# The output gate's state half, formed once and added by VectorE in each batch

## The reference

```
xn = layernorm(x)
x + attention(xn) + cell(xn)

# attention: qkv = xn @ W_qkv + b_qkv, 16 heads of 64, softmax(q k / 8) v, then @ W_out + b_out
# cell: the 8 batches are its time steps, the 512 rows its batch
def step(c, xt):
    ft = sigmoid(xt @ wf.T + c @ uf.T + bf)
    it = sigmoid(xt @ wi.T + c @ ui.T + bi)
    gt = tanh(xt @ wc.T + c @ uc.T + bc)
    return ft * c + it * gt
c_final = scan(step, in_c, xn)
h = tanh(xn @ wo.T + c_final @ uo.T + bo)      # for every time step, with the last state
```

## Time and profile before

| | us |
|---|---|
| median of 3 runs | 822.47 |
| lowest to highest | 821.98 to 822.47 |
| the profiled execution | 821.97 |
| its span in the profile | 820.2 |
| PE busy in it | 811.3 |
| POOL busy | 651.7 |
| DVE busy | 554.4 |
| ACT busy | 481.0 |

### The profile page before, as it was taken

One profiled execution on the slowest core, in us unless ns is written; L12 is line 12 of the kernel. 1 busy time (PEld: TensorE's weight loads), 2 busy tenths in 40 slices (PEclk: granted clock), 3 DMA queues, 4 the chain that ended last, 5 costly groups with the idle time before them and its releaser, 6 DMA issues.

```text
span 820.2 us, 15666 instructions
## 1 busy us (share of the span) xinstructions
PE 811.3 (99%) x5443; PEld 482.3 (59%) x5443; DVE 554.4 (68%) x733; ACT 481.0 (59%) x642; POOL 651.7 (79%) x361
## 2 busy tenths in 40 slices
PE   8899999999999999999999999999999999999998
PEld 5556655575555655556555555557555555666554
DVE  6779768775877647665676657676576757676545
ACT  5646866565556646664666636665566636666352
POOL 4938898895687859887798859988598869988595
PEclk9999999999999999999999999999999999999999
DMA  8102121221101101100001000010001000030010
GB/s 257 53 28 79 28 79 40 53 79 27 41 2 41 28 2 16 35 7 26 1 14 40 1 27 14 1 39 27 1 14 40 1 26 1 14 79 15 2 17 24
DMA packets 81430, 27.00 MB, mean 33 GB/s; under 512 B 63314, under 2 KB 75120, under 8 KB 81392
## 3 DMA queue, kind: packets, MB, share of 16 engines
q1 hardware_dynamic: 81062, 26.35, 13.2%
q10 hardware_dynamic: 330, 0.15, 0.1%
HBM read 16.79 MB, written 8.39 MB: 31 GB/s over the span
## 4 chain that ended last, share of the span: by engine, by line
PE 96%; POOL 1%; ACT 1%; DMA 1%; DVE 0%; ACTq 0%; issue 0%; POOLq 0%
PE st L1048 21%; PE misc L1062 14%; PE pv L1062 14%; PE st L986 10%; PE mx L1034 8%; PE st L1054 7%; PE mx L1100 5%; PE st L1091 4%; PE misc L969 3%; PE mx L969 3%; PE misc L986 3%; PE pv L986 3%; POOL PSUMK L421 1%; POOL PSUMK L428 1%; DMA probs<-in_L_ffn_in_c_dram 1%; PE st L1122 0%
## 5 line engine op out<-in xcount | busy, mean ns | idle before, releaser
L732 DVE TENSOR_REDUCE NM<-mx 128x2 f32<-128x1024 f32 x256 | 313.9, 1226 | 165.0 <-PE mx L1034 165.0
L540 ACT ACTIVATE probs<-st 128x1024 f32<-128x1024 f32 x256 | 256.5, 1026 | 53.6 <-PE st L1054 47.2
L415 POOL TENSOR_TENSOR PSUMK<-probs 128x1024 f32<-128x1024 f32 x64 | 154.1, 2408 | 31.7 <-ACT probs L540 31.7
L421 POOL TENSOR_TENSOR PSUMK<-PSUMK,probs 128x1024 f32<-128x1024 f32 x64 | 153.1, 2392 | 6.6
L428 POOL TENSOR_TENSOR PSUMK<-PSUMK,probs 128x1024 f32<-128x1024 f32 x63 | 151.0, 2396 | 6.4
L407 POOL TENSOR_TENSOR AL<-U,AH 128x512 fp32r<-128x512 f32 x60 | 77.2, 1287 | 81.0 <-ACT AH L532 81.0
L1062 PE MATMUL misc<-probs,VALL 128*64 128x512 f32 x512 | 122.4, 599 | 0.0
L1062 PE MATMUL pv<-probs,VALL 128*64 128x512 f32 x512 | 117.1, 599 | 0.0
L1034 PE MATMUL mx<-KH,QH 64*128 64x512 f32 x512 | 107.5, 413 | 2.0 <-DVE NM L732 1.7
L1048 PE MATMUL st<-QH,KH 64*128 64x512 f32 x512 | 104.0, 399 | 0.3 <-ACT probs L540 0.3
L1048 PE MATMUL st<-QH,KL 64*128 64x512 f32 x512 | 101.8, 390 | 0.0
(11 more groups left out here) (218 smaller groups left out, 1326.1 us busy)
## 6 DMA issues: line engine op xcount, KB each, us to landing
MROW<-TT SPq DMA_DIRECT2D x255, 1.0 KB
x_store<-XH SPq DMA_DIRECT2D x8, 256.0 KB, 2.1
x_store<-XL SPq DMA_DIRECT2D x8, 256.0 KB, 2.4
RX<-R SPq DMA_DIRECT2D x124, 2.0 KB, 1.7
xn_store<-XN SPq DMA_DIRECT2D x7, 256.0 KB, 2.5
XN<-xn_store SPq DMA_DIRECT2D x28, 64.0 KB, 2.3
XSH<-x_store SPq DMA_DIRECT2D x7, 256.0 KB, 2.8
XSL<-x_store SPq DMA_DIRECT2D x7, 256.0 KB, 2.9
```

Of the source, the lines that this page charges most:

```text
L415: nc.gpsimd.tensor_tensor(PSUMK[:, s % 2, :, :], e[:, :, 0, :], e[:, :, 1, :], ALU.add).then_inc(sum_part, 1)
L421: nc.gpsimd.tensor_tensor(PSUMK[:, s % 2, :, :], PSUMK[:, s % 2, :, :], probs[:, s % 2, :, 2, :], ALU.add).then_inc(sum_part, 1)
L540: nc.scalar.activation(probs[:, s % 2, :, u, :], st[:, u % 2, :, :], ACT.Exp, scale=SCALE).then_inc(exp_done, 1)
L732: nc.vector.tensor_reduce(NM[:, s % 2, 0:2 * TB].rearrange("p (h b) -> p h b", h=2)[:, :, b], mx[:, :, :], AX.X, ALU.max, negate=True).the ...
```

## The change

The three products of the output gate with the state are formed once, at the end of batch 1, behind that stretch's sums (`make_state_part`, into mx bank 1). ACT evacuates them with the gate's bias added into tile 0 of XN (`keep_state_part`, in ACT's program behind the last high part of that stretch), and PE waits for this (`part_kept`) before it goes on to the loop and writes mx again. A gate of h is now three matmuls with x alone (`output_gate`). DVE adds the kept array to misc in place (`add_state_part`), and the tanh waits for this addition (`h_added`) instead of the gate and has no bias of its own.

```diff
+        state_part = XN[:, 0, :, :].rearrange("p b d -> p (b d)")
...
             def tanh_h(count, out=OT):
-                act.wait_ge(h_done, count)
-                nc.scalar.activation(out[:, :], misc[:, :], ACT.Tanh, bias=bcol[:, B_O:B_O + 1]).then_inc(ht_done, 1)
+                act.wait_ge(h_added, count)
+                nc.scalar.activation(out[:, :], misc[:, :], ACT.Tanh).then_inc(ht_done, 1)
+
+            def keep_state_part():
+                act.wait_ge(part_made, 1)
+                nc.scalar.activation(state_part, mx[:, 1, :], ACT.Identity, bias=bcol[:, B_O:B_O + 1]).then_inc(part_kept, 1)
...
+            def add_state_part(count):
+
+                dve.wait_ge(h_done, count)
+                dve.wait_ge(part_kept, 1)
+                nc.vector.tensor_tensor(misc[:, :], misc[:, :], state_part, ALU.add).then_inc(h_added, 1)
...
+                    if beside_out and r == N:
+                        add_state_part(n if last else n - 1)
+                    if last and j == 0:
+                        add_state_part(N - 2)
+                    if last and j == 2:
+                        add_state_part(N)
                     if not (first and j == 0):
                         for a in range(2):
                             fill_divisors(n, j, t, a)
...
+            def output_gate(hi, lo):
+
+                for i, (stationary, moving) in enumerate([(gwH[:, 3, :], hi), (gwL[:, 3, :], hi), (gwH[:, 3, :], lo)]):
+                    last = nc.tensor.matmul(misc[:, :], stationary, moving, start=(i == 0), stop=(i == 2))
+                last.then_inc(h_done, 1)
+
+            def make_state_part():
+
+                pe.wait_ge(state_hi, N + 1)
+                pe.wait_ge(state_lo, N + 1)
+                for i, (stationary, moving) in enumerate([(gwH[:, 7, :], DH), (gwL[:, 7, :], DH), (gwH[:, 7, :], DL)]):
+                    last = nc.tensor.matmul(mx[:, 1, :], stationary, moving[:, :], start=(i == 0), stop=(i == 2))
+                last.then_inc(part_made, 1)
...
-                            recurrence(3, XH[:, 0, :], XL[:, 0, :], h_done, N)
+                            output_gate(XH[:, 0, :], XL[:, 0, :])
...
-                        recurrence(3, XH[:, 1, :], XL[:, 1, :], h_done, N)
+                        output_gate(XH[:, 1, :], XL[:, 1, :])
...
-                        recurrence(3, XSH[:, :], XSL[:, :], h_done, N)
+                        output_gate(XSH[:, :], XSL[:, :])
...
                         four_sums(t)
+                        if r == N - 1:
+                            make_state_part()
                         values(n, t + 1, s + 1, (2, 3))
+                        if r == N - 1:
+                            pe.wait_ge(part_kept, 1)
```

More of the change, by code:

```diff
@@ L185, in build_block @@
         four_done, four_turned, four_inverted = sem("four_done"), sem("four_turned"), sem("four_inverted")
+        part_made, part_kept, h_added = sem("part_made"), sem("part_kept"), sem("h_added")
         d_xn, d_xg = sem("d_xn"), sem("d_xg")
@@ L633, in step @@
                         hi_out(n, t - 2, s - 2)
+                    if cell_step(n, j) == N - 1:
+                        keep_state_part()
                     if first and j == 1:
```

## The result

The changed kernel takes **826.88 us** (median of 5 executions, 825.50 to 827.12), the kernel before 822.47 beside it: a ratio of **1.0054, 95% interval 1.0042 to 1.0066**. It is slower, by about 4.4 us. The execution that was profiled took 825.50 us with a span of 823.7.

A forecast was written before the change was run, and what follows sets the result against it. PE is busy 99% of the span, but at six gates the projection waits for DVE's reduction. 0 + 0.60 + 2.02 + 0.80 = +3.42 us on a base of 822.2 gives 825.6 us, range 823.0 to 827.4.

The forecast's parts named there:

- Six gates: Second stretches of batches 2 to 7: the projection still waits for DVE's reduction, so three fewer matmuls gain nothing.
- First stretch of the last batch: The addition queues on DVE behind four lo parts, so misc is ready 0.60 us later instead of 0.68 earlier.
- the nearest row: Price for DVE's addition, taken from forget, which reads mx and state and writes mx: 691 ns.
- I see no reason for a change without it: Assumption that the gate's tanh still takes 688 ns when its bias is gone.
- Third stretch: Last batch: the addition waits on DVE behind all four maxima blocks, so the four sums start 2.02 us later.
- The 1.08 us that the forecast quotes: Last batch, third stretch, before the change: the sums start this long after their load could have, waiting for GpSimd.
- State part: End of batch 1: three matmuls added once on PE behind the sums, with no wait, cost 0.80 us.
- rival 4: DVE's addition in the last batch costs 1.29 us, twice 0.60 more: 826.8; chance 0.05.
- rival 3: The last batch's third-stretch stall is absorbed by something behind it: 0.80 + 0.60 = 1.40, 823.6; chance 0.09.
- the cheap row: The forget operation on DVE, one input in PSUM and one in SBUF, 691 ns, used to price the addition.
- The dear price of 1.29 us: Upper end for DVE's addition, taken from an addition with two SBUF inputs.
- rival 5: PE idles 3.0 us in the last batch's third stretch and the clock falls to 1.2 GHz: about 828; chance 0.04.

The follow-up runs named there:

- Experiment 2: Changed kernel with whole six-matmul gates and the biased tanh again in the last batch's first and third stretches: 823.00 us, ratio 1.0013.
- experiment 8: Changed kernel with the last batch's additions earlier on DVE and, in batches 2 to 7, value products ahead of the projection: 820.48 us, ratio 0.9978.
- Experiment 3: Kernel before, with the tanh in the last batch's third stretch waiting for DVE's transpose behind all reductions: 825.19 us, ratio 1.0036.
- experiments 6 to 8: Value products between gate and projection in second stretches: in the changed kernel 823.90 us, in the kernel before 824.77, in the changed kernel with earlier additions 820.48.
- experiment 1: Changed kernel run again with no edit: 827.50 us, ratio 1.0070.

## Why the prediction was right, point by point

The forecast of 825.6 us with a range of 823.0 to 827.4 held the median, and an execution at full clock comes within 0.1 us of it. Its steps, in the profiled execution:

- **Six gates, 0 us: right.** The delay goes from 1.12 to 1.11 us over five of them and stays at 1.57 over the sixth; the load stays 1.28 us behind the start of the reduction. Experiment 2 shows it in the time and experiment 8 turns it round: where PE has other work there, the gates count.
- **First stretch of the last batch, +0.60: right in its mechanism, 0.42 to 0.46 measured.** Misc is 739.59 - 738.06 - 1.11 = 0.42 us later by this stretch alone, the sums 1.57 - 1.11 = 0.46. The addition does start right behind the last lo part, at 738.22, which is 0.08 us before that part's row ends (737.56 + 0.74); the forecast had added the whole row. It takes 0.67 to 0.69 us as the nearest row said, but the tanh takes 0.60 us and not 0.69. "I see no reason for a change without it" was the weak sentence: the bias as an operand is what the 0.09 us were. Experiment 2 has both forms in one trace, 687 ns with it and 598 without. The Trainium skill, ScalarE: Activation LUTs, What ACT_TABLE_LOAD costs, puts such an operand at about 93 ns; 688 ns against 598 here agree.
- **Third stretch, +2.02: right.** Misc was forecast 2.31 us later than before from this stretch alone and stands at 791.70 - 787.91 - 1.57 = 2.22; the sums 3.53 - 1.57 = 1.96. Experiment 3 gives 1.9 to 2.4 with no matmul removed. PE's own work behind it takes the delay to the end, as the forecast had read from the chain, and GpSimd's release is gone. The 1.08 us that the forecast quotes is idleness of the weight loads; PE itself lost about 0.3 us there before (790.04 against 787.91 + 1.82), which is what its sum in fact uses.
- **State part, +0.80: 0.89 measured.** The three matmuls follow one another as forecast (245.50, 245.83, 246.07), but the step from the last to the value products at 246.39 is 0.32 us and not 0.228. That is the change of kind that shows again in experiments 6 to 8.
- **The addition's price (rival 4) and the absorbed stall (rival 3): out.** Its 0.67 us is the cheap row's; the delay reached the end. The dear price of 1.29 us isn't one of two inputs in SBUF as such: in the trace of before the sum of TG and state, all in SBUF, takes 0.69 us at 739.02, and the eight of the row that the forecast read take 0.69 to 3.58. What makes them long wasn't tried.
- **The clock (rival 5): its chance of 0.04 was far too low, and its price too high.** The forecast took the clock as staying up, since the earlier trace rows show it up in all slices. But there PE never stands still for that long behind the start, so they had nothing to say on it. In 10 of 11 executions of the changed kernel the mean clock was below 1.000, and the profile that shows where has it right behind the stall. It costs 1.3 to 1.7 us; rival 5 had 2.4 on top of the forecast. Its own working, half of 3.0 us of idleness, gives 1.5 and so 827.1, inside the range; the step to "about 828" had no row. The median is the forecast's sum with this added, and the range held it by luck: its upper end had been set for a dearer addition, not for the clock.

Two parts stay open. Why an idleness of 2.85 us leaves the clock up in one execution and takes it down in the next wasn't tried apart. Nor was the fall at the program's start, ahead of which PE waited 1.46 us for a DMA in that profile; 1 of 41 executions of the kernel before beside the experiments has a mean clock of 0.998 too, with 824.02 us.

## What to carry to other kernels

A matmul taken out beside a wait wins nothing until something else is put in its place: ask for each removal which semaphore the next instruction waits for, and by how much it was late. If a sum is moved from the engine that bounds to another, look where it lands in that engine's queue; here the place of two additions cost 4.4 to 5.6 us, about what all 24 matmuls take (5.5). And a new stall of 2 to 3 us on TensorE should be priced with half-speed work behind it (1.3 to 1.7 us here, in most executions), not by its length alone.

## What the runs showed of the hardware

- The granted clock fell to the level of 1.2 GHz after 2.34 us (experiment 3) and 2.85 us (experiment 1) of idleness, but not in every execution; the work behind ran at that level for some 3 us, which cost 1.3 to 1.7 us. Matmuls that nothing needs, put into the stall, kept it up there in the profiled execution.
- It also fell at 8 to 12 us in one profile (0.67 and 0.50), where the kernel is still loading; PE had waited 1.46 us for a DMA just before.
- A tanh of 128x512 takes 598 ns without and 688 ns with its bias operand.
- A change between fp32r products of the gate or projection and the fp32 value passes costs about 0.1 to 0.2 us on a full PE: 0.32 us from the one to the other instead of 0.228 within the first kind, and 2.4 us for an order with twelve more changes.
